# Graph network on one core: lags and engine orders of the edge passes reset, more places for two buffers, half of an attribute load moved to ScalarE

## The reference

```python
x = _layernorm(x + L0(x, edges))                 # attention without a maximum
x = _layernorm(x + L1(x, edges, edge_attr_64))   # GIN with edge features
x = _layernorm(x + L2(x, edge_attr_3, edge_weight, src, dst))   # directions and a radial MLP
x = _layernorm(x + L3(x, src, dst))              # softmax over the edges of a node, per channel
# L0: msg = V[src] * exp(clip(sum(K[src] * Q[dst]) / 4, -5, 5)), summed over dst, divided by the sum of scores
# L1: messages = (x[src] + relu(attr @ W1e + b1e) @ W2e + b2e) * weight[edge], summed over dst
# L2: w = silu(silu(emb @ w0 + b0) @ w1 + b1) @ w2 + b2, four products of w, up(x)[src] and the direction, summed
# L3: a = f_src[src] + f_dst[dst]; e = leaky(a); m = f_v[src] * softmax(e over dst), summed over dst
```

## Time and profile before

| | us |
|---|---|
| median of three runs | 5890.41 |
| profiled execution | 5895.59 |
| its span, first to last instruction | 5893.8 |
| PE busy | 4003.9 (68%) |
| DVE busy | 3942.8 (67%) |
| ACT busy | 3019.7 (51%) |
| POOL busy | 3806.1 (65%) |

### The profile page before, as it was taken

One profiled execution on the slowest core, in us unless ns is written; L12 is line 12 of the kernel. 1 busy time (PEld: TensorE's weight loads), 2 busy tenths in 40 slices (PEclk: granted clock), 3 DMA queues, 4 the chain that ended last, 5 costly groups with the idle time before them and its releaser, 6 DMA issues. The chain is left out here.

```text
span 5893.8 us, 110375 instructions
## 1 busy us (share of the span) xinstructions
PE 4003.9 (68%) x23105; PEld 3440.7 (58%) x23106; DVE 3942.8 (67%) x9753; ACT 3019.7 (51%) x7943; POOL 3806.1 (65%) x3836
## 2 busy tenths in 40 slices
PE   1544444443666666666888888867788887799993
PEld 1444444442555555554666666657777777677772
DVE  5666666666444444465777787757777777688888
ACT  1244444442222222245666666636767777677774
POOL 1577777774777777735777777617777777434343
PEclk9877887785777777787988998989999999899997
DMA  3444444442333333311111111127777777677772
GB/s 90 150 157 157 148 156 156 157 146 58 76 78 79 77 77 77 79 30 58 55 55 55 55 54 55 50 90 255 260 265 261 255 259 263 212 247 250 248 249 99
DMA packets 451724, 824.76 MB, mean 140 GB/s; under 512 B 121837, under 2 KB 223619, under 8 KB 451365
## 3 DMA queue, kind: packets, MB, share of 16 engines
q1 hardware_dynamic: 304872, 469.72, 23.8%
q0 software_dynamic: 141696, 349.47, 20.2%
q10 hardware_dynamic: 5052, 4.43, 0.3%
HBM read 677.74 MB, written 143.81 MB: 139 GB/s over the span
## 5 line engine op out<-in xcount | busy, mean ns | idle before, releaser
L938 DVE TENSOR_TENSOR acc<-acc,banks 128x256 f32 (+2 forms) x4400 | 1609.5, 366 | 926.2 <-PE banks L917 549.1
L917 PE MATMUL banks<-e_msg,e_sel 128*128 128x256 f32 (+1 forms) x5280 | 1178.5, 370 | 9.2 <-DVE acc L938 3.8
L917 PEld LDWEIGHTS banks<-e_msg,e_sel 128*128 128x128 f32 x5280 | 944.9, 210 | 95.6 <-issue 5.2
L855 POOL DMA_INDIRECT e_rows<-kv_t,e_index x800 | 783.5, 979 | 243.7 <-issue 239.7
L855 POOL DMA_INDIRECT e_rows<-x_t,e_index x800 | 778.9, 974 | 243.8 <-issue 238.3
L855 POOL DMA_INDIRECT e_rows<-up_t,e_index x800 | 777.3, 972 | 243.8 <-issue 239.2
L855 POOL DMA_INDIRECT e3m_rows<-fsv_t,e3m_index x800 | 766.1, 958 | 243.7 <-issue 239.1
L891 ACT ACTIVATE e_away<-node_iota,local 128x128 f32<-128x128 f32 x2640 | 839.8, 388 | 7.9 <-issue 1.4
L1016 PE MATMUL banks<-acc,e_sel_t 128*128 x1760 | 308.9, 330 | 586.8 <-DVE e_sel_t L983 574.1
L1107 ACT ACTIVATE e_rows<-banks,e_rows 128x128 f32<-128x128 f32 x880 | 251.6, 369 | 883.9 <-PE banks L1098 434.5
L1016 PEld LDWEIGHTS banks<-acc,e_sel_t 128*128 128x128 f32 x1760 | 267.6, 233 | 623.3 <-issue 622.8
(11 more groups left out here) (197 smaller groups left out, 7756.2 us busy)
## 6 DMA issues: line engine op xcount, KB each, us to landing
e_near<-near_d SPq DMA_DIRECT2D x440, 258.0 KB, 4.5
edge_rows<-e3m_rows SPq DMA_DIRECT2D x220, 512.0 KB, 5.7
e_rows<-edge_rows SPq DMA_DIRECT2D x220, 512.0 KB
e3m_near<-near_d SPq DMA_DIRECT2D x220, 258.0 KB, 5.0
e_attr<-in_attr_rows SPq DMA_DIRECT2D x880, 32.0 KB
e_rows<-kv_t,e_index POOLq DMA_INDIRECT x800
e_rows<-x_t,e_index POOLq DMA_INDIRECT x800
e_rows<-up_t,e_index POOLq DMA_INDIRECT x800
```

Of the source, the lines that this page charges most:

```text
L855: G.indirect_dma_start(out=self.rows[:, u, i, 0:self.width], out_offset=None, in_=self.table, in_offset=bass.IndirectOffsetOnAxis(ap=index ...
L917: m = PE.matmul(bank[n_bank][:, col + at:col + at + rows.shape[1]], self.place_of_sel(g)[:, i, :], rows, start=True, stop=True)
L938: V.tensor_tensor(to, to, bank[n_bank][:, col:col + self.sums].unsqueeze(1), ALU.add).then_inc(self.s_added[i], 1)
```

## The change

It has these parts. `ByNode` takes a number of places for `sel_t`; e0 gives five, e3m keeps two. `scatter` can be emitted in two parts. e0: sums go from lag 5 to 6, halved around the queries at lag 3 (before 2); on DVE turn stands ahead of the adds. e1: sums and adds are in the same step, select has lag 1 and stands ahead of the adds, and two of the four attribute loads of a group are issued by ACT. e2: h2 has five places, distance and at_zero lag 6 and ahead of silu1 and silu2, and DVE's list is reordered. e3m: all lags but those of gather and turn go up by one or two, and DVE's list starts with leaky and scan. e3 and the node phases are as before. Core of the diff:

```diff
-        def scatter(self, g, parts):
-
-            for i in range(GROUP):
+        def scatter(self, g, parts, items=range(GROUP)):
+
+            for i in items:
...
+        def __init__(self, ps, s_used, places=2):
+            self.ps, self.s_used, self.places = ps, s_used, places
+            self.sel_t = ps.sb("sel_t", [P, places, GROUP, P])
...
-            by_node = ByNode(ps, s_q)
+            by_node = ByNode(ps, s_q, SPAN)
...
-            def sums(g):
+            def sums_a(g):
                 PE.wait_ge(s_msg, g.upto(0))
                 PE.wait_ge(ps.s_sel, g.upto(0))
-                ps.scatter(g, lambda i: [(0, msg[:, g.at(SPAN), i, :])])
-
-            ps.run([(0, gather), (2, queries_to_edges), (5, sums), (6, ps.add(0)), (4, message),
-                    (6, ps.add(1)), (3, products), (6, ps.add(2)), (3, dot), (6, ps.add(3)), (3, score),
-                    (1, by_node.turn), (3, distance), (3, at_zero)])
+                ps.scatter(g, lambda i: [(0, msg[:, g.at(SPAN), i, :])], (0, 1))
+
+            def sums_b(g):
+                ps.scatter(g, lambda i: [(0, msg[:, g.at(SPAN), i, :])], (2, 3))
+
+            ps.run([(0, gather), (6, sums_a), (3, queries_to_edges), (6, sums_b), (3, distance), (3, at_zero),
+                    (1, by_node.turn), (6, ps.add(0)), (4, message), (6, ps.add(1)), (3, products), (6, ps.add(2)),
+                    (3, dot), (6, ps.add(3)), (3, score)])
...
+                attributes(g, SP, SP_ENGINE, (0, 1))
+
+            def attributes(g, engine, kind, items):
                 u = g.at(SPAN)
                 _, chunks = nc.values_load_multi_w_load_instructions(
-                    chunk_of[0:1, ds(g.n * GROUP, GROUP)], engines=(SP_ENGINE,), min_val=0, max_val=N_CHUNKS - 1,
-                    skip_runtime_bounds_check_because=CLIPPED)
+                    chunk_of[0:1, ds(g.n * GROUP + items[0], len(items))], engines=(kind,), min_val=0,
+                    max_val=N_CHUNKS - 1, skip_runtime_bounds_check_because=CLIPPED)
                 if g.old(SPAN):
-                    SP.wait_ge(s_h, g.upto(-SPAN))
-                for i in range(GROUP):
-                    SP.dma_start(attr[0:ED, u, i, :], a["attr_rows"][ds(chunks[i], 1), :, :]
-                                 .rearrange("a k e -> (a k) e")).then_inc(s_attr[u], 16)
+                    engine.wait_ge(s_h, g.upto(-SPAN))
+                for i, chunk in zip(items, chunks):
+                    engine.dma_start(attr[0:ED, u, i, :], a["attr_rows"][ds(chunk, 1), :, :]
+                                     .rearrange("a k e -> (a k) e")).then_inc(s_attr[u], 16)
+
+            def attributes_by_act(g):
+                attributes(g, A, ACT_ENGINE, (2, 3))
             def hidden(g):
                 PE.wait_ge(s_attr[g.at(SPAN)], (g.turn(SPAN) + 1) * 64)
@@ -1114,8 +1124,8 @@
                 ps.have_rows(PE, g)
                 ps.scatter(g, lambda i: [(0, ps.row(g)[:, i, 1:])])
-            ps.run([(0, gather), (1, hidden), (3, sums), (2, weighted), (4, ps.add(0)), (4, ps.add(1)),
-                    (4, ps.add(2)), (4, ps.add(3)), (0, ps.select)])
+            ps.run([(0, gather), (1, hidden), (3, sums), (2, weighted), (0, attributes_by_act), (1, ps.select),
+                    (3, ps.add(0)), (3, ps.add(1)), (3, ps.add(2)), (3, ps.add(3))])
...
-            h2 = ps.sb("h2", [RH + 1, 2, 4 * P])
+            h2 = ps.sb("h2", [RH + 1, SPAN, 4 * P])
...
-                    (2, silu1), (4, silu2), (5, distance), (5, at_zero), (6, by_direction), (6, by_scalars), (6, dot),
-                    (8, ps.add(0)), (6, m1), (8, ps.add(1)), (6, m2), (8, ps.add(2)), (6, m3), (8, ps.add(3))])
+                    (6, distance), (6, at_zero), (2, silu1), (4, silu2),
+                    (6, by_direction), (6, dot), (6, by_scalars), (6, m1), (6, m2), (6, m3),
+                    (8, ps.add(0)), (8, ps.add(1)), (8, ps.add(2)), (8, ps.add(3))])
...
-            ps.run([(0, gather), (4, keep), (2, both_ends), (4, forward), (6, backward), (8, sums),
-                    (3, take), (7, only_last), (6, distance), (6, at_zero), (5, scan), (9, ps.add(0)), (9, ps.add(1)),
-                    (9, ps.add(2)), (9, ps.add(3)), (4, resets), (3, leaky), (1, by_node.turn)],
+            ps.run([(0, gather), (5, keep), (10, sums), (3, both_ends), (5, forward), (7, backward),
+                    (9, only_last), (4, take), (8, distance), (8, at_zero),
+                    (4, leaky), (6, scan), (10, ps.add(0)), (5, resets), (10, ps.add(1)), (10, ps.add(2)),
+                    (10, ps.add(3)), (1, by_node.turn)],
```

More of the change, by code:

```diff
@@ L51 @@
 PE_ENGINE = mybir.EngineType.PE
+ACT_ENGINE = mybir.EngineType.Activation
 SP_ENGINE = mybir.EngineType.SP
@@ L958, in build @@
     class ByNode:
-        def __init__(self, ps, s_used):
-            self.ps, self.s_used = ps, s_used
+        def __init__(self, ps, s_used, places=2):
+            self.ps, self.s_used, self.places = ps, s_used, places
             self.near = ps.sb("near", [P, SPAN, GROUP, P + 1])
-            self.sel_t = ps.sb("sel_t", [P, 2, GROUP, P])
+            self.sel_t = ps.sb("sel_t", [P, places, GROUP, P])
             self.s_near = [ps.sem(f"near{u}") for u in range(SPAN)]
@@ L980, in turn @@
             self.here(V, g)
-            if g.old(2):
-                V.wait_ge(self.s_used, g.upto(-2))
-            V.tensor_scalar(self.sel_t[:, g.r2], self.near[:, g.at(SPAN), :, 1:], node_step[:], None, ALU.is_equal
+            if g.old(self.places):
+                V.wait_ge(self.s_used, g.upto(-self.places))
+            V.tensor_scalar(self.sel_t[:, g.at(self.places)], self.near[:, g.at(SPAN), :, 1:], node_step[:], None, ALU.is_equal
                             ).then_inc(self.s_t, 1)
@@ L1015, in queries_to_edges @@
                 for i in range(GROUP):
-                    m = PE.matmul(bank[B_Q[g.r2]][:, i * P:(i + 1) * P], by_node.sel_t[:, g.r2, i, :],
+                    m = PE.matmul(bank[B_Q[g.r2]][:, i * P:(i + 1) * P], by_node.sel_t[:, g.at(by_node.places), i, :],
                                   side(ds(tiles[i], 1)).rearrange("p a d -> p (a d)"),
@@ L1193, in silu2 @@
                 A.wait_ge(s_h2, g.upto(0))
-                if g.old(2):
-                    A.wait_ge(s_w, g.upto(-2))
+                if g.old(SPAN):
+                    A.wait_ge(s_w, g.upto(-SPAN))
                 for h in range(2):
                     units = slice(h * RH, (h + 1) * RH)
-                    m = A.activation(h2[0:RH, g.r2, h * 2 * P:(h + 1) * 2 * P], hidden_bank(g, 1)[units, :], ACT.Silu,
+                    m = A.activation(h2[0:RH, g.at(SPAN), h * 2 * P:(h + 1) * 2 * P], hidden_bank(g, 1)[units, :], ACT.Silu,
                                      bias=b1[units, :])
@@ L1206, in weights @@
                 for i in range(GROUP):
-                    m = PE.matmul(bank[B_W[g.r2]][:, i * P:(i + 1) * P], h2[:, g.r2, i * P:(i + 1) * P], w2[:],
+                    m = PE.matmul(bank[B_W[g.r2]][:, i * P:(i + 1) * P], h2[:, g.at(SPAN), i * P:(i + 1) * P], w2[:],
                                   start=True, stop=True)
@@ L1309, in both_ends @@
                     PE.matmul(to, ident[:], ps.row(g)[:, i, 0:D], start=True, stop=False)
-                    m = PE.matmul(to, by_node.sel_t[:, g.r2, i, :],
+                    m = PE.matmul(to, by_node.sel_t[:, g.at(by_node.places), i, :],
                                   side(ds(tiles[i], 1)).rearrange("p a d -> p (a d)"),
@@ L1409, in to_edges @@
                 for i in range(GROUP):
-                    m = PE.matmul(bank[B_M[g.r2]][:, i * P:(i + 1) * P], by_node.sel_t[:, g.r2, i, :],
+                    m = PE.matmul(bank[B_M[g.r2]][:, i * P:(i + 1) * P], by_node.sel_t[:, g.at(by_node.places), i, :],
                                   acc[:, ds(tiles[i], 1), 0:D].rearrange("p a d -> p (a d)"),
```

## The result

The changed kernel took 5923.89 us (median of five runs, 5923.54 to 5928.62) beside 5890.41 us for the kernel before in the same five rounds: ratio 1.0059, 95% interval 1.0044 to 1.0074. That is 33.5 us slower, on the side that the text held likeliest and inside its range, but above the forecast's own 5891 to 5914 and 2.7 times the 12.6 us of the sum. The profiled execution has a span of 5926.2 us, 32.4 more than before.

What follows compares the result with a forecast made beforehand. GpSimd, issuing gathers without pause, was taken to bound the gathering passes. Tails +8 and +1.6 and lengthening -8, +8 and +3 gave +12.6 us, laid on the median of 5890.4: 5903 us, range 5862 to 5938.

Steps and rivals of the forecast that it cites:

- the sum: Whole kernel: tails +8 and +1.6, gather lengthening -8, +8 and +3, together +12.6 us.
- The floor: Gathering passes: 1.246 us a gather, 4.98 us a group, so no pass's gathers take under 1096.5 us.
- The first step: Gathering passes: GpSimd waits for nobody, so waits removed on other engines are worth 0 on the stretch of gathers.
- e2, VectorE's order: VectorE's step in e2 grows from 3.85 to 5.0 us, adding 8 us behind the last gather (+7 to +10).
- e2's gathers: Two-input instructions in e2 shift against gather starts; lengthening 22.1 us before, 28 at random: +3 us.
- The rival that VectorE becomes the bound: e2: VectorE's step exceeds GpSimd's 5.107 us; at 5.2 it adds 20 us, giving 5922 us; chance 0.13.
- e0: End of e0: one more VectorE step ahead of the last group's products, +1.6 us (0 to 3.3).
- e1: e1: selects overlap fewer gather starts as catching up behind boundaries shrinks, -8 us (bounds 0 and the whole 23.7).
- e3m: e3m: moved resets lengthen gathers; 9.3 us unlikely to be kept, 35 with starts at random; value +8 us.
- the random price: Gathering passes: mean lengthening with VectorE starts at random; e0 35, e1 25, e2 28, e3m 35 us.
- The rival of contention at random: Gathering passes: starts at any offset to gathers, lengthening 123 against 82 us (+41), giving 5941 us; chance 0.15.
- Contention falls: Gathering passes: a rigid phase clears gather starts, saving up to 82 us; half, -41, gives 5859 us; chance 0.22.

Runs made afterwards that it cites:

- e3m_lags_only: The changed kernel with e3m's new lags but VectorE's old order in e3m (scan, four adds, resets, leaky, turn); ratio 1.0033 to the kernel before.
- e2_adds_spread: The changed kernel with VectorE's list of e2 as before, adds between m1, m2 and m3; ratio 1.0045 to the kernel before.
- e3m_resets_last: The changed kernel with e3m's resets behind the fourth add instead of the first; 7262.05 us, ratio 1.0244 to the kernel before; 1.0074 when run again elsewhere.
- e0_turn_and_scores: The changed kernel with e0's message product reading scores from PSUM and ScalarE building e0's transposed selection; ratio 1.0017 to the kernel before.
- e1_select_on_act: The changed kernel with e1's selection matrix built by ScalarE in two steps instead of by VectorE; ratio 1.0030 to the kernel before.

## Why the prediction was right, and where its sizes were off

*The floor held.* The first step, that GpSimd waits for nobody and that no wait removed is worth anything, was confirmed by the idle time that did not move and by e3m_lags_only and e2_adds_spread. No gather stretch fell under its floor.

*e2, VectorE's order.* Value 8 us behind the last gather, measured 5.3 (and 7.0 back when undone), so 31.9 us where 33 to 36 were named. The step was taken as 5.0 us and is 4.83, just under the 4.9 to 5.1 named, which is 1.2 us over the seven steps; the other 1.6 us come from group 212, whose product by scalars now starts 13.13 us ahead of the end of the last gather and not 11.55, since the long wait at the boundary ahead of it is gone. In the step, m1 behind by_scalars costs 0.11 us as the lower end had it (3837.17 - 3836.86 = 0.31 where 0.20 was), the load of tile numbers costs nothing. The rival that VectorE becomes the bound was out of reach, by 0.29 us a step.

*e2's gathers.* Value +3, measured +2.7 in the profile of the result. In seven other runs that keep e2's new list (without e3m_resets_last) they took 1126.8 to 1131.5 us, 3 to 8 more than in the one profile before, on chips where the kernel before took 2.5 to 10.5 us more as well: the size is uncertain by that.

*e0.* +1.6 predicted, +1.4 measured, of it 1.2 behind the last gather.

*e1.* The step that failed is "those that overlap a start come from the catching up behind a boundary, which shrinks". PE's waits for the attributes were cut in two and not in sum (370.6 us in 40 waits before, 371.2 us in 80 after, in the 800 gathers of the loop), and selects that follow the arriving rows overlap starts too: 105 gathers under L877 and 26.9 us, where 109 and 25.7 had been. Value -8, measured +1.1 in the gathers. The mean went from 974 to 975 ns, which is the text's own sign that this term has the wrong sign.

*e3m.* The mis-sized term, and the one that made the result: +8 taken, +23.9 measured. The text had the mechanism, the pass and the sign (9.3 us "is unlikely to be kept") and gave 35 us for starts at random; the 800 gathers now have 790.8 - 800 x 0.946 = 34.0 us. So the random price was right for the sum of this pass and I took a third of the way to it. That it came out so near is in part luck: for 220 groups it gives 28 us under the resets and 11 under turn, and there were 19.3 and 15.8; and a cost that returns in six profiles and goes with the place of one stage is not at random. I had no row for a lower value: with a before that is well below the random price, and an order that is not kept, the random price would have been the better estimate. The text also argued from the resets alone and left out turn (0.5 us), which is in its 35 us: one gather under it before and 88 after.

*The rival of contention at random* was therefore true of one pass: of its +41 us the 25.7 of e3m came (24.7), in the pass where the phase had been good; e0, e1 and e2 stayed within 1.6, 1.5 and 4.2 us of what they were. Contention falls, with 0.22, had no row behind it but e3m's luck before the change.

## What to carry to other kernels

Where one engine is busy or in its fixed gap all the time, look at the duration of its instructions before any wait: the spread between median and mean of one group, times its count, is what is left to gain or lose in that stretch, and here it had a cause on another engine that the timeline can name. Work of VectorE with two SBUF inputs beside a GpSimd that sets the pace had a price here although VectorE was idle a third of the time: put one input into PSUM, or give the work to ScalarE. Removing waits between engines that are not the bound gained nothing here, and a block of dependent adds in place of adds spread over other work lengthened what had to be drained behind the last gather.

## What the runs showed of the hardware

Where counts are given, they are over the eleven profiles of this case without e3m_resets_last. In them 5111 gathers took more than 0.965 us, and all but some 30 are of the kinds below.

- The disturbance can be removed wholly: no gather of e0 took more than 0.963 us (e0_turn_and_scores) and none of e1 more than 0.966 us (e1_select_on_act) once the products with two SBUF inputs and the 128x512 tensor-scalar are off VectorE. The clip on 32 elements a partition (0.17 us) stayed there in e0 and lengthened nothing.
- A gather is sensitive at its start, by the overlap less 0.13 us (0.22 us gave 0.09 at 4514.36, 0.45 gave 0.32 in the earlier trace rows). The same rule comes out of all of them: for 3410 products and selections with two SBUF inputs (0.55 and 0.69 us long, overlap above 0.15 us, started at least 0.1 us ahead) the difference is 0.127 us on average, and for 96% of them between 0.123 and 0.133; for 720 turns (started at least 0.12 us ahead) it is 0.128.
- A product with two SBUF inputs that starts within a gather costs nothing: 7865 such starts, the longest gather 0.974 us. The fp32 tensor-scalar does when it starts 0.34 to 0.49 us in (1.05 us at 713.01).
- An instruction with one input in PSUM (L1057 at 707.66, 0.68 us over the start of a gather) costs nothing at the same duration: 251 starts under this product in three runs, the longest gather 0.963 us. The reductions and the scan cost nothing either: 4064 starts, the longest 0.962 us.
- An add that waits for the one before on the same engine cost about 0.25 us more to the next start than one between independent work, and a product right behind its input 0.11 us.
- Between 0.49 and 0.66 us into a gather it is the tensor-scalar that pays, and the gather does not. Turn usually takes 0.48 us. In all 530 cases in which it started in this stretch of a gather that itself took under 0.965 us, it took over 0.5 us, up to 0.71, and ended 1.19 to 1.22 us behind the gather's start, just ahead of the next gather. In e3m 109 of 219 turns took over 0.5 us before the change and 47 of 220 after it: before, VectorE paid, and it had time. In the changed kernel's e3m, for one:

```profile
4726.30 0.95 POOL L856 DMA_INDIRECT e3m_rows<-fsv_t,e3m_index  x1 [0.30 <-issue]
4726.78 0.71 DVE L984 TENSOR_SCALAR e3m_sel_t<-e3m_near,node_step 128x512 f32<-128x512 f32 x1
```
